# Moving a recurrence's background jobs between its leaves: grams, centering, deviations, state decays and the output projection

## What is computed

```python
def step(S, t):                       # S: heads x 128 x 128, t runs over 2048 tokens
    q_t, k_t, v_t, a_t, b_t = t
    y = jnp.einsum('bhvk,bhk->bhv', S, k_t)
    err = y - v_t
    S = a_t[..., None] * S - (b_t[..., None] * err)[..., None] * k_t[:, :, None, :]
    o = jnp.einsum('bhvk,bhk->bhv', S, q_t)
    return (S, o)
```

## Time and profile before

| | us |
|---|---|
| median of three runs | 3618.18 |
| lowest and highest | 3605.82, 3619.48 |
| the profiled execution, device time | 3618.45 |
| its span, first to last instruction | 3616.7 |
| busy in the span: TensorE, VectorE, ScalarE, GpSimd | 3084.4, 2423.8, 1603.2, 1247.2 |
| mean granted clock of TensorE | 0.911 |

### The profile page before, as it was taken

How to read it: one execution, slowest core, us unless ns; L and a number is a source line. 1 busy time by engine, 2 the same in 40 slices (tenths; PEclk the granted TensorE clock), 3 DMA queues, 4 the chain that set the end, 5 groups by cost and what they waited for, 6 DMA issues and landing times. The chain is left out here.

```text
span 3616.7 us, 48221 instructions
## 1 busy us (share of the span) xinstructions
PE 3084.4 (85%) x14200; PEld 2208.0 (61%) x14200; DVE 2423.8 (67%) x4820; ACT 1603.2 (44%) x3478; POOL 1247.2 (34%) x1452
## 2 busy tenths in 40 slices
PE   5999997488888888888888888888888888878888
PEld 3555554366666667666766766667666766634444
DVE  5777776577777777787777777777787776522222
ACT  3666665254544444444444444444444444311110
POOL 1666666233433333333333333333333333300000
PEclk9999999698989898898998989889898988889999
DMA  1656556422121122121212221122221211020000
GB/s 68 261 203 239 221 222 242 105 53 42 37 47 37 36 55 43 36 49 36 48 29 56 44 41 37 36 56 42 40 45 36 55 25 30 14 85 18 18 17 17
DMA packets 431891, 255.04 MB, mean 71 GB/s; under 512 B 400080, under 2 KB 414128, under 8 KB 416944
## 3 DMA queue, kind: packets, MB, share of 16 engines
q1 hardware_dynamic: 431680, 252.42, 25.5%
HBM read 147.40 MB, written 104.99 MB: 70 GB/s over the span
## 5 line engine op out<-in xcount | busy, mean ns | idle before, releaser
L245 DVE SCALAR_TENSOR_TENSOR A_acc<-A_psY,A_w,A_acc 128x410 f32<-128x410 f32 (+1 forms) x720 | 419.2, 637 | 156.0 <-ACT A_acc L285 156.0
L767 POOL TENSOR_TENSOR B_WT<-B_WT,B_G 128x128 f32<-128x128 f32 (+2 forms) x224 | 168.0, 750 | 977.4 <-issue 551.1
L1067 ACT ACTIVATE B_WL<-B_psT 128x128 f32<-128x128 f32 (+2 forms) x480 | 150.1, 313 | 633.6 <-PE B_psT L1473 633.6
L345 PE MATMUL A_psY<-A_xT,A_w 128*128 128x413 f32 (+1 forms) x960 | 347.2, 510 | 9.0 <-PE A_psAG L351 7.7
L980 DVE TENSOR_TENSOR B_NC<-B_NC,B_psM 128x256 f32<-128x256 f32 x480 | 199.8, 416 | 216.6 <-PE B_psM L1497 172.2
L202 POOL TENSOR_TENSOR A_outs<-A_outs,A_acc 128x410 f32<-128x410 f32 (+1 forms) x240 | 229.4, 987 | 254.1 <-ACT A_outs L293 254.1
L345 PEld LDWEIGHTS A_psY<-A_xT,A_w 128*128 128x128 f32 x960 | 180.2, 189 | 165.4 <-issue 164.2
L1067 ACT ACTIVATE B_PQ<-B_psM 128x64 f32<-128x64 f32 (+2 forms) x480 | 125.7, 262 | 308.5 <-DVE B_NC L980 304.5
L983 DVE TENSOR_REDUCE B_W<-B_NC 128x64 f32<-128x320 f32 x512 | 248.8, 486 | 17.6
L1473 PE MATMUL B_psT<-ident,B_WT 128*128 128x128 f32 x384 | 113.8, 296 | 165.8 <-DVE B_WT L985 165.8
L1497 PE MATMUL B_psM<-B_BD,B_WL 128*128 128x128 f32 x1536 | 242.1, 301 | 13.4
(11 more groups left out here) (194 smaller groups left out, 7300.9 us busy)
## 6 DMA issues: line engine op xcount, KB each, us to landing
scr<-A_outs SPq DMA_DIRECT2D x48, 1024.0 KB, 5.5
B_KQ<-scr SPq DMA_DIRECT2D x96, 512.0 KB, 6.5
scr<-A_outag SPq DMA_DIRECT2D x32, 1024.0 KB, 8.1
A_xc<-nbeta SPq DMA_DIRECT2D x18, 1024.0 KB, 8.6
scr<-A_x SPq DMA_DIRECT2D x16, 1024.0 KB, 7.6
B_A<-scr SPq DMA_DIRECT2D x32, 512.0 KB, 5.5
B_C<-scr SPq DMA_DIRECT2D x32, 512.0 KB, 4.5
B_G<-scr SPq DMA_DIRECT2D x32, 512.0 KB, 4.4
```

Source lines behind the costliest of these rows:

```text
L245: nc.vector.scalar_tensor_tensor(a, y, w[:, s, col:col + 1], a, ALU.mult, ALU.add)\
L345: last = nc.tensor.matmul(psY[p][:, y0:y0 + HALO + t1 - t0], wp[:, p, kt, :], xT[:, kt, t0:t1 + HALO], start=kt == 0, stop=kt == KT - 1)
L767: tt(dst, dst, gr, ALU.mult).then_inc(wsc.sem, 1)
L1067: copy = lambda out, in_: nc.scalar.activation(out, in_, ACT.Copy)
```

## The change

TensorE's jobs are dealt out anew over the leaves, the consumers on VectorE and ScalarE move with them, and GpSimd waits at the start of a chunk (psc0, counted up by VectorE's `scale_leaf`) before its first scaling. No operation is added or taken away.

```diff
--- before.py
+++ after.py
@@ -361,18 +361,19 @@
     first, last, out, wo = g == 0, g + 1 == NCH, g > 0, g % 2 and g >= 3
     jobs = {0: out and [("qk", 0), ("qk", 1)],
             1: [("own", 1, 0), ("own", 1, 1)],
-            2: (out and [("qk", 2)] or []) + [("gram", 1)],
-            3: (out and [("qk", 3)] or []) + [("decay", 0), ("decay", 1)],
-            4: [("kk", 1, 0), ("kk", 1, 1)] + (out and [("qk", 4)] or []),
+            2: [("gram", 1)] + (out and [("qk", 2)] or []),
+            3: out and [("qk", 3), ("qk", 4)],
+            4: [("kk", 1, 0), ("kk", 1, 1), ("gram", 4)],
             5: out and [("oc", 0)],
-            6: [("gram", 4)] + (out and [("oc", 1)] or []),
-            8: (out and [("oc_rest", 1)] or []) + [("gram", 5)],
-            9: ([] if last else [("own", 0, 0), ("own", 0, 1)]) + [("decay", 2), ("decay", 3)],
-            10: (out and [("var", 0)] or []) + [("ktok", 0), ("ktok", 1)],
+            6: out and [("oc", 1)],
+            7: out and [("oc_rest", 1)],
+            8: [("gram", 5)],
+            9: [] if last else [("own", 0, 0), ("own", 0, 1)],
+            10: (out and [("var", 0)] or []) + [("decay", 0), ("decay", 1)],
             11: [] if last else [("kk", 0, 0), ("kk", 0, 1)],
-            12: [] if last else [("gram", 0)],
-            13: (wo and [("wo", 0)] or []) + (out and [("rstd", 0), ("rstd", 1)] or []),
-            14: wo and [("wo", 1)]}
+            12: ([] if last else [("gram", 0)]) + (wo and [("wo", 0)] or []),
+            13: [("ktok", 0), ("ktok", 1)] + (wo and [("wo", 1)] or []),
+            14: (out and [("rstd", 0), ("rstd", 1)] or []) + [("decay", 2), ("decay", 3)]}
     return jobs.get(j) or []
 
 
@@ -770,6 +771,7 @@
             for g in range(NCH):
                 gates = lambda *parts: [gate(g - 2, n) for n in parts if g >= 2]
                 queries = lambda *parts: [decayed_q(g - 1, n) for n in parts if g]
+                wait(pool, psc0, g, 1)
                 scale_right(g, 1)
                 scale_right(g, 3)
                 queries(0, 1)
@@ -996,48 +998,48 @@
                         mask_own(g, 1, 0)
                         mask_own(g, 1, 1)
                     elif j == 3:
+                        mask_gram(g, 1)
                         if g:
                             y_terms(g - 1, 2)
-                        mask_gram(g, 1)
-                    elif j == 4:
-                        if g:
-                            y_terms(g - 1, 3)
-                        decay_state(g, 0)
-                        decay_state(g, 1)
+                    elif j == 4 and g:
+                        y_terms(g - 1, 3)
+                        y_terms(g - 1, 4)
                     elif j == 5:
                         row_pairs(here)
-                        if g:
-                            y_terms(g - 1, 4)
+                        mask_gram(g, 4)
                     elif j == 6:
                         leaf_solution(here, 1)
                     elif j == 7:
                         leaf_solution(here, 2)
                         leaf_solution(here, 3)
-                        mask_gram(g, 4)
                     elif j == 9:
-                        mask_gram(g, 5)
                         if more:
                             decays(g + 1)
+                        mask_gram(g, 5)
                     elif j == 10 and more:
                         mask_own(g + 1, 0, 0)
                         mask_own(g + 1, 0, 1)
                     elif j == 11:
-                        decay_state(g, 2)
-                        decay_state(g, 3)
+                        decay_state(g, 0)
+                        decay_state(g, 1)
                     elif j == 12:
                         if g:
                             invert(g - 1)
                         if more:
                             row_pairs(nxt)
-                    elif j in (13, 14) and more:
-                        leaf_solution(nxt, j - 12)
+                    elif j == 13 and more:
+                        leaf_solution(nxt, 1)
+                        mask_gram(g, 0)
+                    elif j == 14:
+                        if more:
+                            leaf_solution(nxt, 2)
+                        if g % 2 and g >= 3:
+                            att_sum((g - 3) // 2)
                     elif j == 15:
-                        if more:
-                            mask_gram(g, 0)
                         if g:
                             norm(g - 1)
-                        if g % 2 and g >= 3:
-                            att_sum((g - 3) // 2)
+                        decay_state(g, 2)
+                        decay_state(g, 3)
 
                     if j < JM:
                         scale_leaf_w(g, j)
@@ -1277,27 +1279,30 @@
                         centered_copy(g - 1, 0)
                     elif j == 7 and more:
                         decay_copies(g + 1)
-                    elif j == 8 and more:
-                        leaf_keys(2 * g + 2)
+                    elif j == 8:
+                        if more:
+                            leaf_keys(2 * g + 2)
+                        if g:
+                            centered_copy(g - 1, 1)
                     elif j == 9 and g:
-                        centered_copy(g - 1, 1)
                         squares(g - 1)
                     elif j == 10 and more:
-                        sort_keys(2 * g + 2)
+                        leaf_diagonals(2 * g + 2)
                     elif j == 11:
+                        if more:
+                            sort_keys(2 * g + 2)
+                        if g:
+                            deviation(g - 1)
+                    elif j == 12 and more:
+                        sort_queries(2 * g + 2)
+                    elif j == 14:
                         for i in range(2):
                             ps = take_bank(act, g, "ktok", i)
                             wait(act, stu, g, 0)
                             copy(KTOK[:, 4 * i:4 * i + 4, :].rearrange("p n c -> p (n c)"), ps[:]).then_inc(ktok.sem, 1)
-                        if g:
-                            deviation(g - 1)
                         if more:
-                            sort_queries(2 * g + 2)
-                    elif j == 12 and more:
-                        leaf_diagonals(2 * g + 2)
-                    elif j == 14 and more:
-                        block_keys(2 * g + 2)
-                    if j == 14 and g % 2 and g >= 3:
+                            block_keys(2 * g + 2)
+                    if j == 13 and g % 2 and g >= 3:
                         att_copy((g - 3) // 2)
                 wait(act, wt, g, J)
                 wait(act, wsc, g, JM // 2)
```

## The result

The changed kernel takes 3454.86 us (median of 4 runs, 3452.55 to 3461.74), the kernel before 3613.72 us beside it: a ratio of 0.9565 [0.9539, 0.9591], 159 us less. Forecast were 140 us less, 3478 us. The profiled execution took 3461.74 us (span 3460.0).

What follows compares the result with a forecast made beforehand. No engine was the bound alone: leaf by leaf, TensorE's jobs or VectorE's work ended last. Gains of 6.6 us in 16 even chunks and 2.3 in 15 odd ones made 140 us, 3618 to 3478; range 3425 to 3590.

Steps and rivals of the forecast that it cites:

- Start of a chunk: GpSimd's new wait puts its scaling behind VectorE's leaf-0 work: 0.6 us a chunk gained, bounds 0 and 0.85.
- Leaves 1 to 5: TensorE's jobs swapped for others of equal length, VectorE's moved work covered by them: nothing gained.
- leaves 6 and 7: Gram 4 leaves leaf 6 and oc_rest enters leaf 7: 0.17 us a chunk gained.
- Leaf 8: Only gram 5 is left there, 2.68 us instead of a mean of 6.61: gain 3.93 a chunk, the largest term.
- Leaf 9: The decays no longer wait for gram 5: 5.28 us for 5.38, gain 0.1 a chunk.
- leaves 10 and 11: More idle time ahead and the clock falling: 11.3 us for a mean of 10.38, loss 0.9 a chunk.
- Even chunks: Without output projection: 0.6 us lost to gram 0's mask in leaf 13, 3.3 gained at the end, gain 2.7.
- Odd chunks: Projection moved to leaves 12 and 13: 3.0 us lost in leaf 12, 1.4 gained at the end, net -1.6.
- Rival 1: Clock stays low at even chunks' ends and in leaves 10 and 11: only 62 us faster, 3556; chance 0.21.
- Rival 2: Sixteen transposes replace wo in leaf 14, clock falls at odd chunks' ends too: 24 us slower, 3642; chance 0.09.
- Rival 3: GpSimd's products end 2 us late at the turn of a chunk: 62 us lost, 3540; chance 0.08.
- Rival 4: The leaf-8 gain is taken back by an unseen wait, the change does nothing: 3618; chance 0.07.

Runs made afterwards that it cites:

- no_gpsimd_wait: The changed kernel without GpSimd's wait for psc0 at the start of a chunk: 3464.43 us.
- mask_behind_y: The changed kernel with gram 1's mask in leaf 3 put back behind `y_terms` on VectorE: 3475.95 us.
- fill_products: The changed kernel with seven float32 products that nobody reads added on TensorE behind leaf 9's job: 3398.23 us.
- state_decays_early: The changed kernel with the last two state decays moved back to leaves 10 (TensorE) and 11 (VectorE): 3509.63 us.
- split_decays: The changed kernel with VectorE's three decay products spread over leaves 9, 10 and 11, ScalarE's readers moved with them: 3340.98 us.
- fill_transposes: The changed kernel with fourteen transposes that nobody reads added on TensorE behind leaf 9's job: 3397.90 us.

## Why the prediction came out as it did

The time lay in the range, 23 us below the number, and faster had been given 0.84. Step by step:

- *Start of a chunk* (0.6): right in its mechanism and mis-sized, 0.2 to 0.4 by the table and 0.3 by no_gpsimd_wait. A part was lost again to another part of the change: behind the last state decays GpSimd is late, and the chunk's first L982 takes 0.68 us in the mean instead of 0.43.
- *Leaves 1 to 5* ("Nothing"): wrong, 0.6 us a chunk, some 19 us. The prediction looked at TensorE's jobs, whose lengths are equal, and took VectorE's order as covered. Leaf 3's merge reads gram 1 and had waited for its mask; ahead of `y_terms` the mask is in time. mask_behind_y shows it with 21 us. That is leaf 3, 0.4 of the 0.6 us (4.07 to 3.66); the 0.2 us of leaf 4 (3.89 to 3.67) aren't the mask's, and no run tried them. The 0.17 us of leaves 6 and 7 didn't come, 9.25 us before and after.
- *Leaf 8* (3.93): its length came as predicted, 2.82 us for 2.68. As an account of what pays, this is the step that failed. It credits the move of oc_rest with 3.93 and the order of the decays with 0.1 in leaf 9. Alone in the kernel before, the two are worth 4.5 and 4.9 us from T7 to T12, and undoing the first makes the changed kernel 40 us faster. The prediction saw VectorE wait 3.38 us for gram 5 in leaf 8, and didn't ask what the decays would do in that time once they stood ahead of the mask; nor that the move takes that time away.
- *Leaf 9* (5.28) and *leaves 10 and 11* (11.3): both as measured, 5.20 and 11.3. The 11.3 was a value chosen between two rows and not derived, so that it came out to the tenth is luck. Its reason, more idle time before T10 (2.06 us in the mean for 1.43), is shown by fill_products.
- *Even chunks* (2.7): 3.5. T13 to T14 lost 0.3 and not the mask's 0.6, and the end took 13.26 for 13.75. The clock does fall in leaf 14, for one stretch of 3.4 us (1890.30 to 1893.70, 0.50), which the estimate of 0.9 us was meant for.
- *Odd chunks* (-1.6): -1.3, with leaf 12 at 5.70 and the end at 11.74.
- *Rival 1* is false, since the even ends came up. *Rival 2* is false: none of the 13 odd ends of chunks 5 to 29 fell to the lower clock, all are at 1.00. *Rival 3* names a real overlap; the price was 0.3 us a chunk for the 2 of the rival. *Rival 4* is false.

Of what it said would show it, T8 to T9, the missing wait for gram 5, L985 of leaf 0 (0.28), the wait of 2 us before T10, odd T12 to T13 and even ends under 14.5 are all there. The number was good because the sum was made over the whole change, in which the two parts' overlap was counted once; the split of that sum between them was not. It was also helped by errors that cancel in part, 0.3 us too much at the start of a chunk against 0.6 left out in leaves 3 and 4.

What stays open: where state_decays_early lost the 20 us that its trace doesn't hold; what the two parts are worth together with the state decays left in leaf 9; and why the clock still falls in most chunks of split_decays, where TensorE hardly waits before T10.

## What to carry to other kernels

When a change moves a long job of one engine to another step, ask what other engines did beside it: it may have been the cover of the next step's work, and the parts of such a change should be tried alone, as their gains needn't add up. Work that several steps can take, such as three dependent products, is better spread over them than kept together. A wait that costs nothing by itself can cost later through TensorE's clock, so read the clock of the stretch behind it before calling it free.

## What the hardware showed that was not expected

- Work that nobody reads, 1.7 us in each of 31 chunks, made the kernel 57 us faster (1.6%), since it held the granted clock up behind it: leaves 10 and 11 are at 0.81 in 23 of the 27 chunks, where the changed kernel has 0.57 or 0.68 in all.
- For this, transposes count as products do: 3397.90 and 3398.23 us. In the changed kernel the stretch at 1890.30, which runs the transposes of rstd and of the decays, is at 0.50 and the one behind it at 1.00. These are float32 transposes of 128x128. The Trainium skill (TensorE: Matmul & The Clock Gate, Part 4: PE-mode transpose) has it that transpose mode doesn't count as busy in the same way and that the full clock doesn't come up for it. These runs don't agree; by that rule fill_transposes would have stood near the changed kernel's 3454.86.
- Sixteen one-column matmuls took 3.57 us behind a wait of 2.03 and 2.03 us in the earlier trace rows. The profile counts them as busy, the engine is 97% busy through leaves 10 and 11 (10.33 of 10.69 us), and the clock is low all the same: a busy share near one doesn't tell that the clock is up.
